# Attention output brought to the projection by VectorE block transpositions and a GpSimd product, in a shifted-window transformer block

## The reference, cut to what matters

```
y   = roll(layernorm(x, g1, b1), (-2, -2))          # then cut into windows
q, k, v = split(y @ qkv_w + qkv_b)                  # 4 heads of 8 channels
attn = softmax(q * 8**-0.5 @ k.T + rel_bias + mask) # 128 x 128 for each window and head
o   = (attn @ v) @ proj_w + proj_b                  # 32 -> 32
x   = x + roll_back(o)
z   = gelu(layernorm(x, g2, b2) @ fc1_w + fc1_b) @ fc2_w + fc2_b
return x + z
```

## Time and profile before

| | |
|---|---|
| median of three runs | 245.58 us |
| the profiled execution | 244.59 us |
| its span, first to last instruction | 242.8 us |
| mean granted TensorE clock | 0.968 |
| TensorE busy (matmuls) | 213.5 us, 88% |
| TensorE weight loads | 121.5 us, 50% |
| VectorE busy | 166.4 us, 69% |
| ScalarE busy | 148.4 us, 61% |
| GpSimd busy | 110.2 us, 45% |
| row maxima on VectorE, 64 of 1.221 us | 78.0 us |
| exponentials on ScalarE, 64 of 1.022 us | 65.4 us |

### The profile page before, as it was taken

One profiled execution on the slowest core, in us unless ns is written; L12 is line 12 of the kernel. 1 busy time (PEld: TensorE's weight loads), 2 busy tenths in 40 slices (PEclk: granted clock), 3 DMA queues, 4 the chain that ended last, 5 costly groups with the idle time before them and its releaser, 6 DMA issues.

```text
span 242.8 us, 8095 instructions
## 1 busy us (share of the span) xinstructions
PE 213.5 (88%) x3344; PEld 121.5 (50%) x3344; DVE 166.4 (69%) x268; ACT 148.4 (61%) x219; POOL 110.2 (45%) x77
## 2 busy tenths in 40 slices
PE   0176489899999999999999999999999999988983
PEld 0143233465565556655665665566556655533331
DVE  5856546575886879687868785777676666557553
ACT  8362235666774777576667766766545665597660
POOL 6636982164309841891388068520801430403500
PEclk9999657999999999999999999999999999999998
DMA  6828635545504632263264035304610000001222
GB/s 196 224 67 255 183 126 180 176 136 178 155 7 155 196 99 74 84 188 109 90 185 125 10 123 165 113 9 156 199 49 1 4 5 5 3 0 43 96 107 102
DMA packets 25495, 26.57 MB, mean 109 GB/s; under 512 B 3744, under 2 KB 22944, under 8 KB 25344
## 3 DMA queue, kind: packets, MB, share of 16 engines
q1 hardware_dynamic: 24356, 25.08, 32.9%
q10 hardware_dynamic: 1104, 0.99, 1.5%
HBM read 17.01 MB, written 8.78 MB: 106 GB/s over the span
## 4 chain that ended last, share of the span: by engine, by line
issue 35%; PE 34%; POOL 19%; DVE 4%; ACT 3%; DMA 2%; ACTq 1%; POOLq 0%; DVEq 0%
PE pav L856 5%; POOL rstd L341 5%; PE ps L823 5%; POOL parts L355 4%; POOL xc L333 4%; PE ps L836 3%; PE ps L791 3%; PE ps L873 2%; POOL yn L348 2%; PE pch L935 2%; POOL X L361 2%; PE pav L887 2%; PE pch L923 2%; ACT prob L653 2%; PE ps L809 2%
## 5 line engine op out<-in xcount | busy, mean ns | idle before, releaser
L454 DVE TENSOR_REDUCE negm<-ps 128x8 f32<-128x1024 f32 x64 | 78.0, 1221 | 29.2 <-PE ps L809 28.9
L653 ACT ACTIVATE prob<-ps 128x1024 f32<-128x1024 f32 x64 | 65.4, 1022 | 28.8 <-PE ps L836 28.8
L341 POOL TENSOR_TENSOR rstd<-var,neghalf 128x16 f32<-128x16 f32 x16 | 47.0, 2936 | 73.5 <-DVE var L425 73.4
L823 PE MATMUL ps<-rel_j,id_b 96*32 96x512 bf16 x512 | 40.1, 387 | 2.3 <-ACT prob L653 2.3
L856 PE MATMUL pav<-prob,va 128*32 128x128 f32 x1024 | 41.2, 279 | 0.0
L856 PEld LDWEIGHTS pav<-prob,va 128*32 128x32 f32 x1024 | 24.1, 109 | 13.1 <-issue 6.3
L809 PE MATMUL ps<-k_rows,q_rows 64*128 64x128 bf16 x512 | 25.9, 223 | 4.1 <-DMA k_rows<-slots 4.0
L791 PE MATMUL ps<-rel_i,ident_b 64*64 64x512 bf16 x256 | 27.2, 415 | 0.2 <-DVE negm L454 0.2
L836 PE MATMUL ps<-q_rows,k_rows 64*128 64x128 bf16 x512 | 25.6, 220 | 0.1
L355 POOL TENSOR_TENSOR parts<-rest,parts 128x512 bf16<-128x512 f32 x16 | 18.5, 1159 | 15.2 <-ACT parts L637 15.2
L648 ACT ACTIVATE m_hi<-pq 16x128 bf16<-16x128 f32 x32 | 8.4, 264 | 25.7 <-PE pq L779 25.7
(11 more groups left out here) (108 smaller groups left out, 308.3 us busy)
## 6 DMA issues: line engine op xcount, KB each, us to landing
slots<-parts SPq DMA_DIRECT2D x24, 256.0 KB, 2.5
q_rows<-slots SPq DMA_DIRECT2D x42, 128.0 KB
k_rows<-slots SPq DMA_DIRECT2D x42, 128.0 KB
X<-x_tok SPq DMA_DIRECT2D x8, 256.0 KB, 3.7
y_tok<-res SPq DMA_DIRECT2D x7, 256.0 KB, 2.0
q_rows<-slots SPq DMA_DIRECT2D x12, 64.0 KB, 2.4
k_rows<-slots ACTq DMA_DIRECT2D x12, 64.0 KB, 2.5
q_rows<-m_hi SPq DMA_DIRECT2D x32, 4.0 KB
```

The costliest lines, as they stand in the source:

```text
L341: pool.tensor_tensor(rstd[:, i, :], var[:, i, :], neghalf[:], ALU.pow).then_inc(rstd_done[i], 1)
L454: dve.tensor_reduce(dst, first_home(j)[:].rearrange("p (a u n) -> p a u n", u=2, n=TOK), AX.X, ALU.max, negate=True).then_inc(max_done, 1)
L653: act.activation(prob[:, j % NPROB, :], ps2[:], ACT.Exp).then_inc(exp_done, 1)
L823: pe.matmul(ps2[32 * c:32 * (c + 1), 512 * e:512 * (e + 1)], id3_b[0:96, :], rel_j[0:96, c, e].unsqueeze(2).to_broadcast([96, 2, 2, TOK]), ...
```

## The change

`pav` is no longer copied and transposed on TensorE. VectorE's block transposition, which turns each 32x32 block of fp32 in place of a full transposition, reads `pav` and writes `o_blocks`: within each strip of 32 partitions and each 32 columns, tokens and rows change places. So a partition holds tokens of one head, and the reciprocal and the product can be taken along the columns. The reciprocal stays on VectorE, reading SBUF. The product moves to GpSimd and writes `onorm` in the same wide layout (128x512, the unused columns cleared once at the start). A second block transposition on VectorE brings it back to channels on partitions, as `onT` (128x512). As the rows are not packed any more, the projection takes four matmuls in place of two, each with 128 columns of `onT` as stationary operand and a 128x64 weight as the moving one.

The steps now stand: VectorE transposition and reciprocal in slots 1 and 5, GpSimd product in slots 1 and 5, VectorE's second transposition in slots 2 and 6, projection and added attention in slots 3 and 7. ScalarE has no part in it. GpSimd's power for the first norm moves from slot 4 to slot 5, behind the product.

```diff
-               g2=1, b2=1, fc1b=1, fc2b=1, vb=1, wv=128, wp=128, ...
+               g2=1, b2=1, fc1b=1, fc2b=1, vb=1, wv=128, wp=64, ...
@@ GpSimd
+            pool.memset(onorm[:], 0.0).then_inc(on_zero, 1)
+            def normalize(q):
+                pool.wait_ge(rec_done, q + 1)
+                after(pool, onT_done, q)
+                pool.tensor_tensor(onorm[:].rearrange("p (n d) -> p n d", d=16)[:, :, 0:HD],
+                                   o_blocks[:].rearrange("p (n d) -> p n d", d=16)[:, :, 0:HD],
+                                   rec[:].unsqueeze(2).to_broadcast([128, 32, HD]), ALU.mult).then_inc(on_done, 1)
+                if p % 4 == 1 and 0 <= (p - 5) // 4 < OCTETS - 1:
+                    normalize((p - 5) // 4)
-                if s == 4 and b + 3 < B:
+                if s == 5 and b + 3 < B:
                     power(first_norm(b + 3))
@@ VectorE
-            def normalize(q):
...
+            def tokens_first(q):
+                dve.wait_ge(av_done, 4 * q + 4)
                 after(dve, on_done, q)
+                dve.transpose(o_blocks[:], pav[:]).then_inc(o_done, 1)
+                dve.wait_ge(o_done, q + 1)
+                dve.reciprocal(rec[:].unsqueeze(2),
+                               o_blocks[:].rearrange("p (n d) -> p n d", d=16)[:, :, HD:HD + 1]).then_inc(rec_done, 1)
+            def channels_first(q):
+                dve.wait_ge(on_done, q + 1)
+                after(dve, proj_done, q)
+                dve.transpose(onT[:], onorm[:]).then_inc(onT_done, 1)
-                if p % 4 == 0 and 0 <= (p - 8) // 4 < OCTETS:
-                    add_attention((p - 8) // 4)
+                if p % 4 == 3 and 0 <= (p - 7) // 4 < OCTETS:
+                    add_attention((p - 7) // 4)
+                if p % 4 == 1 and 0 <= (p - 5) // 4 < OCTETS:
+                    tokens_first((p - 5) // 4)
                 if s == 1 and 3 <= b + 3 < B:
                     dve.wait_ge(d_x[b + 3], 16)
                     means(first_norm(b + 3), b + 3)
                 if p % 4 == 2 and 0 <= (p - 6) // 4 < OCTETS:
-                    normalize((p - 6) // 4)
+                    channels_first((p - 6) // 4)
@@ ScalarE: the copies to onT (slots 3, 7) and oT (slots 1, 5) go
@@ TensorE
-            def tokens_first(q):
...
-            def channels_first(q):
...
+            def project_out(q):
+                pe.wait_ge(onT_done, q + 1)
                 after(pe, x2_done, q)
                 for u in range(4):
+                    mm = pe.matmul(pch[:, 64 * u:64 * (u + 1)], onT[:, 128 * u:128 * (u + 1)], P("wp"),
                                    start=True, stop=True)
                 mm.then_inc(proj_done, 1)
                 if p % 4 == 3 and 0 <= (p - 7) // 4 < OCTETS:
-                    channels_first((p - 7) // 4)
-                if p % 4 == 0 and 0 <= (p - 8) // 4 < OCTETS:
-                    project_out((p - 8) // 4)
+                    project_out((p - 7) // 4)
-                if p % 4 == 2 and 0 <= (p - 6) // 4 < OCTETS:
-                    tokens_first((p - 6) // 4)
@@ the tail: the last octet goes the same new way; octet 14 is done within the loop
             weighted_values(PAIRS - 1)
-            tokens_first(OCTETS - 1)
             fc1(1)
             fc2(0)
-            channels_first(OCTETS - 1)
+            project_out(OCTETS - 1)
             fc1(2)
-            project_out(OCTETS - 1)
@@ the packed projection weight
+    for h in range(HEADS):
+        for wi in range(2):
+            at = 32 * h + 16 * wi
+            wp[at:at + HD, C * wi:C * (wi + 1)] = p["proj_w"][HD * h:HD * (h + 1)]
```

More of the change, by code:

```diff
@@ L34 @@
 _WIDTHS = dict(g1=1, b1=1, qkb=1, qks=1, colscale=128, wqk=128, ident=128,
[L35 removed]
+               g2=1, b2=1, fc1b=1, fc2b=1, vb=1, wv=128, wp=64, wpb=C, pb=C, w1=F, w2=C, id3=32)
 PCOL, _at = {}, 0
@@ L99, in swin_kernel @@
         prob = sb("prob", [128, NPROB, 1024])
-        oT = sb("oT", [128, 512])
+        o_blocks = sb("o_blocks", [128, 512])
         rec = sb("rec", [128, 32])
-        onorm = sb("onorm", [128, 256])
-        onT = sb("onT", [128, 256])
+        onorm = sb("onorm", [128, 512])
+        onT = sb("onT", [128, 512])
         mT2 = sb("mT2", [128, 512])
@@ L397, in _ @@
                     power(second_norm(b - 1))
+            normalize(OCTETS - 1)
             i, seq = second_norm(B - 1)
@@ L538, in _ @@
             remainder(1, 1, pch[:])
[L540 to L548, removed]
             for p in range(FIRST, PAIRS):
@@ L704, in _ @@
                         middle_part(n, s // 2 - 1)
[L705 to L709, removed]
                 if s == 5 and 1 <= b + 1 < B:
@@ L717, in _ @@
                     copy_yT2(B - 3, Q0)
[L718 to L722, removed]
                 if p % 2 == 0 and 0 <= (p + 2) // 2 < GROUPS:
@@ L846, in weighted_values @@
                 if j % 4 == 0:
-                    after(pe, oT_done, j // 4)
+                    after(pe, o_done, j // 4)
                 if j == 0:
@@ L880, in fc2 @@
                 if m == 0:
-                    pe.wait_ge(oT_done, OCTETS)
+                    pe.wait_ge(o_done, OCTETS)
                 elif m < B - 1:
@@ L917, in _ @@
             pe.wait_ge(ident_ready, 1)
-            def tokens_first(q):
-                pe.wait_ge(oT_done, q + 1)
+            def project_out(q):
+                pe.wait_ge(onT_done, q + 1)
                 after(pe, x2_done, q)
                 for u in range(4):
-                    mm = pe.transpose(pch[:, 128 * u:128 * (u + 1)], oT[:, 128 * u:128 * (u + 1)], P("ident"))
-                mm.then_inc(otok_done, 1)
-            def channels_first(q):
[L927 to L935, removed]
+                    mm = pe.matmul(pch[:, 64 * u:64 * (u + 1)], onT[:, 128 * u:128 * (u + 1)], P("wp"),
                                    start=True, stop=True)
@@ L1072, in _pack @@
         wv[C * wx:C * (wx + 1), C * wx:C * (wx + 1)] = p["qkv_w"][:, 2 * C:]
-    for gp in range(2):
-        for h in range(HEADS):
-            for wi in range(2):
-                at, g = 64 * gp + 16 * h + 8 * wi, 2 * gp + wi
-                wp[at:at + HD, C * g:C * (g + 1)] = p["proj_w"][HD * h:HD * (h + 1)]
+    for h in range(HEADS):
+        for wi in range(2):
+            at = 32 * h + 16 * wi
+            wp[at:at + HD, C * wi:C * (wi + 1)] = p["proj_w"][HD * h:HD * (h + 1)]
     return a
```

19 lines of the change are left out of this document (5 added, 14 removed).

## The result

The changed kernel took 257.14 us (median of 4 runs, 255.42 to 259.23), the kernel before 246.18 beside it: a ratio of 1.050 on record, interval 1.046 to 1.054 (the two medians alone divide to 1.045; slower by either). The forecast was 254 us, in a range of 246 to 261, slower with a chance of 0.73. The profiled execution took 257.69 us.

A forecast was written before the change was run, and what follows sets the result against it. It took TensorE as the bound, with the exponential's and maximum's loops close behind. Heavy images add 7.1 us; with light images, image 0 and the tail the sum is 8.8, giving 254 us, range 246 to 261.

The forecast's parts named there:

- slot 0 to 2: Heavy images 1 to 4: transposition, reciprocal, mean pair and remainder delay slot 1's maximum; 5.71 to 6.46 us, +0.75 each.
- slot 6 to 0: Heavy images: later power in slot 5 delays centring, square and slot 7's exponential; 6.28 to 6.67 us, +0.39 each.
- the tail: At the end, slot 62 loses L923 and the last part's first MLP waits for no transposition; 0.7 us less.
- Slot 4 to 6: Heavy images: VectorE's transposition, reciprocal and variances delay slot 5's maximum; 5.68 to 5.96 us, +0.28 each.
- Slot 2 to 4: Heavy images: projection of 1.0 us in slot 3, then the exponential's loop; 5.16 to 5.51 us, +0.35 each.
- the exponential's loop: Second bias, first bias, scores, exponential and signal hold a slot without extras at 2.41 us, 2.62 with the maxima.
- Light images: Images 5 to 7: projection lengthens slots 3 and 7, emptied slots fall to the 2.41 us loop; +1.0, +0.8, +0.3 us.
- Unit costs: Assumed times: VectorE transposition 0.69 us, eight projection pairs 1.0, GpSimd product some 0.6, clearing of `onorm` hidden.
- TensorE is not the bound: Denies the rival that TensorE's 88% busy share is all that counts, giving 240.5 us; chance 0.12.
- transpositions are not slow: Denies the rival that VectorE's transpositions take 1.22 us each, giving 260 us; chance 0.18.
- the exponential's loop is not all: Denies the rival that VectorE and GpSimd finish in time and only this loop costs, giving 246 us; chance 0.14.

The follow-up runs named there:

- e1: Changed kernel with VectorE's first block transposition on only the left half of `pav` in slots 1 and 5; ratio 1.035 against 1.048 for the changed kernel.
- e5: Changed kernel with ScalarE's copy of `pav` back, the new operations moved to later slots, none ahead of the row maximum in slots 1 and 5; 249.36 us.
- e2: Changed kernel with two of the projection's four matmuls left out; 253.86 us, ratio 1.039.
- e8: Changed kernel with the projection in halves, two matmuls in slots 3 and 7, two in 4 and 0, added attention one slot later; 252.87 us.
- e9: Changed kernel with 128 moving columns for 64 in each projection matmul; projection 1.09 us against 1.04, no difference in the whole.
- e3: Changed kernel with GpSimd multiplying in place of the first norm's power, images 3 to 7; slot 6 to 0 fell from 6.76 to 6.08 us.
- e4: Kernel before with one of the four TensorE transpositions L923 per octet; ratio 0.994, interval 0.990 to 0.997.
- e6: Changed kernel with projection in halves, the second norm's transposition in slot 6, norm steps moved on VectorE, ScalarE and GpSimd; 243.73 us, ratio 0.993 to the kernel before.
- e10: e6 with the second norm's variances moved to slot 1 and GpSimd's product ahead of that norm's power; ratio 1.013 to the kernel before.

## Why the prediction was right

The forecast of 254 us was near 257.14, and the main causes are shown by the experiments. Two terms came near in size by luck (slot 0 to 2 in part, slot 6 to 0 in its last link), and it did not foresee the tail and the low clock. The step sizes, summed over images 1 to 4 from the starts of L779 and L774, forecast and measured.

- **Slot 0 to 2** (VectorE's transposition and reciprocal ahead of the maximum): 3.0 forecast, 3.0 measured. e1 shows the cause. One part of the sum was luck: I put 0.81 us for the mean pair, where my own have 1.37 (129.59 to 130.96), and gave no reason. The changed kernel has 0.75 (136.62 to 137.37), because the GpSimd instruction with which the small one ends is now the short product, and the bias addition comes later (e5). With 1.37 the sum would have been 0.56 us higher in images 2 to 4.
- **Slot 4 to 6**: 1.1 forecast, 1.15 measured; e1 again.
- **Slot 2 to 4** (the projection of eight pairs, then the exponential's loop): 1.4 forecast, 1.4 measured without the low clock; e2, e8 and e9 show it.
- **Slot 6 to 0** (power, centring, square, then by the forecast the exponential): 1.6 forecast, 1.9 measured. e3 shows the chain through the power. Its last link I had wrong: TensorE waits for ScalarE's copy L631 in images 2 to 4 and for the scaled first norm in image 1, and not for the exponential of slot 7. By the exponential, which ended at 132.13, the stretch would have been some 6.6 us, near my 6.67; the copy makes it 6.76. The forecast came near because both stand behind the same square.
- **Light images** 5 to 7: 1.0, 0.8 and 0.3 forecast, 0.92, 0.75 and 0.46 measured. The loop of 2.41 us is seen in all emptied slots (137.76 after 135.35 above).
- **Unit costs**: transpositions 0.72 and 0.70 us (0.69 taken, by the copy), eight pairs 1.04 (1.0 taken), the product 0.63 (0.6), the clearing hidden. The estimate of 1.24 us by the Trainium skill's table (VectorE: DVE Perf Modes, The three transpose paths) does not agree with the trace. The scaling was at fault, and not the page's 311 ns: it takes the fixed part four times, and e1 has 0.18 us of that. With 0.18 and 1.04 ns a column (e1), 128 columns would be 0.31 us.
- **ScalarE** lost its copies and gained the kernel nothing: as costed. The second transposition waited 1.5 us for the product in all 16 octets: no stall, as costed.

The rivals fell: TensorE is not the bound (e4), transpositions are not slow (0.72 us), and the exponential's loop is not all (e1).

**Where it was off** is the tail. I forecast 0.7 us less there; from slot 60's transposition of maxima to the end it took 39.86 us for 39.04. I had octet 14's transposition free to go, and it stands behind image 6's whole second norm on VectorE. The changed kernel's VectorE and TensorE there:

```profile
216.76 0.66 DVE L426 TENSOR_REDUCE ssum<-X 128x16 f32<-128x512 f32 x1
...
219.84 0.17 DVE L436 TENSOR_SCALAR var<-vsum 128x16 f32<-128x16 f32 x1
219.93 0.71 DVE L477 STREAM_TRANSPOSE o_blocks<-pav 128x512 f32<-128x512 f32 x1
```

```profile
220.69 0.64 PE L851 MATMUL pav<-prob,va 128*32 128x128 f32 x16 [1.01 <-DVE o_blocks L477]
```

That this transposition is on the tail's path e1 shows: with half of it TensorE's wait falls from 1.01 to 0.74 us, and the tail from 39.86 to 39.6. e6 has the square and the variances behind that transposition; its tail took 38.4 us, though other things differ there too.

Of the 4.3 us between the forecast of 253.4 and the profiled 257.69, these are 1.5; another 2.4 are a low clock in one stretch, which I had not considered; 0.3 are slot 6 to 0.

## What to carry to other kernels

The share of busy time called TensorE the bound, but an engine's extras can be cover: before taking work off it, write down the loops through the other engines (here second bias, scores, exponential: 2.41 us) and count only what is above them in that slot. Moving work to an engine with 30% idle costs its full length in the slot where it stands ahead of the one result that others wait for (e1: 0.27 us for 0.27), whatever the average says. Name the instruction that waits at the end of a chain from its own row: two results behind the same square came within 0.15 us of each other here. When a step is moved into an idle gap, ask what made the gap: in e10 it went with its cause.

## What I had not expected

**The granted clock fell within the steady stretch, in slots 3 and 4.** The changed kernel by stretches: us, then busy us of each engine, and the clock as a share of 2.4 GHz.

```profile
136.00:140.00 4.00, 2.75 (x55) 1.31 (x56) 3.88 (x8) 1.92 (x3) 3.21 (x4) 1.00 0.46 143
140.00:144.00 4.00, 4.00 (x52) 2.83 (x48) 1.84 (x3) 1.60 (x2) 0.77 (x1) 0.60 0.06 16
```

Ahead of the fall TensorE was busy for 2.75 us of 4, with the wait for the maximum in it; from 140.40 on instructions take up to twice as long (eight projection pairs 1.65 us for 1.10, from the second bias to the maxima 1.02 for 0.54), which is the lower level of 1.2 GHz for most of it. Slot 2 to 4 took 7.95 us (139.30 to 147.25) for 5.55. The second profile of the same kernel had this twice (7.98 and 7.85), e2 and e8 once (6.48 for 5.10 and 6.70 for 5.18), and e1, e3, e5, e6, e9, e10, the kernel before and the runs built on it never. In each case it came behind slot 2's waits, but most slots 2 with the same waits had none of it; what decides it these runs do not show. It cost 2.3 to 2.4 us each time in the changed kernel, 1.4 and 1.5 in e2 and e8, and it may be why the changed kernel's runs spread over 3.8 us (255.42 to 259.23). That is not shown: the mean clock does not tell, as the fastest of them has 0.958 and the profiled one 0.982, and a low stretch ahead of the steady part lowers it too (in the kernel before at 25.5 to 39 us, mean 0.52).
